# VectorE's order in a transformer layer: both duos' maxima first, then reciprocals and block transposes

## The reference, cut to what matters

```
scores = einsum('bthd,bThd->bhtT', q, k) * (1.0 / sqrt(HD))
scores = where(mask, scores, finfo(float32).min)
out    = einsum('bhtT,bThd->bthd', softmax(scores), v) @ Wo
x = x + tanh(g_xattn[0]) * attention(layernorm(x), ctx, mask)
x = x + tanh(g_ffn[0])   * experts(layernorm(x))
```

## Time and profile before

| what | value |
|---|---|
| median of three runs | 627.38 us |
| the profiled execution | 626.95 us, its span 625.1 us |
| TensorE busy (share of span) | 590.8 us (95%) |
| VectorE busy | 406.8 us (65%) |
| ScalarE busy | 272.5 us (44%) |
| GpSimd busy | 309.0 us (49%) |
| granted TensorE clock, mean | 0.99 of full speed |
| chain that ended last, by engine | PE 71%, DVE 13%, issue 4%, ACT 3%, DMA 3%, SPq 3% |

### The profile page before, as it was taken

How to read it: one execution, slowest core, us unless ns; L and a number is a source line. 1 busy time by engine, 2 the same in 40 slices (tenths; PEclk the granted TensorE clock), 3 DMA queues, 4 the chain that set the end, 5 groups by cost and what they waited for, 6 DMA issues and landing times.

```text
span 625.1 us, 10907 instructions
## 1 busy us (share of the span) xinstructions
PE 590.8 (95%) x2882; PEld 343.7 (55%) x2883; DVE 406.8 (65%) x1266; ACT 272.5 (44%) x713; POOL 309.0 (49%) x272
## 2 busy tenths in 40 slices
PE   3899999999999999999999999889999999999993
PEld 2444465555556555555655555446666656666562
DVE  3578978898998989988899976247353222322231
ACT  2765665566565665665655554212412221122210
POOL 3643554565564698565796655412463222222221
PEclk9999999999999999999999989989999999999998
DMA  8944577586777889687686866999576442333312
GB/s 312 328 111 105 115 163 165 126 183 151 165 148 176 170 191 209 131 181 175 162 205 146 176 150 152 285 323 282 117 165 118 66 57 42 49 51 52 46 23 26
DMA packets 113970, 93.72 MB, mean 150 GB/s; under 512 B 38513, under 2 KB 107505, under 8 KB 113905
## 3 DMA queue, kind: packets, MB, share of 16 engines
q1 hardware_dynamic: 91824, 70.37, 46.5%
q10 hardware_dynamic: 15360, 13.64, 9.9%
q0 software_dynamic: 6720, 8.95, 8.5%
HBM read 27.72 MB, written 12.36 MB: 64 GB/s over the span
## 4 chain that ended last, share of the span: by engine, by line
PE 71%; DVE 13%; issue 4%; ACT 3%; DMA 3%; SPq 3%; ACTq 1%; POOLq 0%; POOL 0%; DVEq 0%
PE ps_s L1625 20%; PE ps_o L1439 12%; PE ps_o L1653 9%; PE ps_s L1393 9%; DVE blocksT L1128 5%; PE ps_a L1449 5%; DVE probs L1116 4%; PE ps_t L1336 4%; PE ps_t L1646 2%; PE ps_o L1406 2%; DMA mask<-mask_dram 2%; ACT probs L720 2%; PE ps_t L1393 2%; PE ps_a L1336 1%; SPq L414 1%
## 5 line engine op out<-in xcount | busy, mean ns | idle before, releaser
L595 POOL TENSOR_TENSOR probs<-probs,inv_sum 128x802 f32<-128x802 f32 x128 | 195.2, 1526 | 138.4 <-DVE inv_sum L1105 137.3
L720 ACT ACTIVATE probs<-probs,neg_max 128x401 f32<-128x401 f32 x256 | 159.4, 625 | 107.3 <-DVE neg_max L1116 105.8
L1625 PE MATMUL ps_s<-w_sb,xgT 128*128 x288 | 137.0, 599 | 3.3 <-issue 3.3
L1116 DVE CUSTOM_DVE_ANT_0 probs<-ps_s,biases 128x401 f32<-128x401 f32 x215 | 116.2, 571 | 21.2 <-PE ps_s L1393 14.4
L1128 DVE STREAM_TRANSPOSE blocksT<-probs 128x832 f32<-128x832 f32 x124 | 129.0, 1040 | 0.4 <-POOL probs L595 0.4
L646 POOL DMA_INDIRECT out_dram<-yg,ids x36 | 56.1, 1559 | 147.3 <-DVE yg L1286 136.8
L1439 PE MATMUL ps_o<-probsT,v_sb 128*64 128x512 f32 x496 | 113.6, 600 | 0.0
L1393 PE MATMUL ps_s<-kT,qT 64*128 64x201 f32 (+1 forms) x860 | 109.6, 350 | 3.5 <-DVE neg_max L1116 2.8
L1393 PEld LDWEIGHTS ps_s<-kT,qT 64*128 64x128 f32 x860 | 84.9, 188 | 44.1 <-issue 27.2
L858 ACT COPY gatedT<-ps_t 128x512 f32<-128x512 f32 x36 | 21.1, 586 | 150.7 <-PE ps_t L1646 150.7
L1276 DVE TENSOR_TENSOR gated<-ps_s,silu 128x512 f32<-128x512 f32 x36 | 24.9, 691 | 91.9 <-PE ps_s L1625 87.5
(11 more groups left out here) (167 smaller groups left out, 515.7 us busy)
## 6 DMA issues: line engine op xcount, KB each, us to landing
probsT<-blocksT SPq DMA_DIRECT2D x276, 96.0 KB
probsT<-blocksT SPq DMA_DIRECT2D x92, 128.0 KB
probsT<-blocksT ACTq DMA_DIRECT2D x96, 96.0 KB
xg_blocks<-x_regrouped SPq DMA_DIRECT2D x156, 32.0 KB, 2.1
probsT<-blocksT ACTq DMA_DIRECT2D x32, 128.0 KB
w_sb<-W1T_dram SPq DMA_DIRECT2D x8, 512.0 KB, 5.1
w_sb<-W2T_dram SPq DMA_DIRECT2D x8, 512.0 KB, 6.2
w_sb<-W3T_dram SPq DMA_DIRECT2D x8, 512.0 KB, 8.0
```

The lines of the kernel that those rows point to most:

```text
L595: pool.tensor_tensor(duo, duo, inv_sum[:, u:u + 2].unsqueeze(2).to_broadcast([P, 2, LASTK]), ALU.mult)\
L720: act.activation(probs[:, b, 0:LASTK], probs[:, b, 0:LASTK], ACT.Exp, bias=neg_max[:, b:b + 1], scale=-1.0, accum_out=sum_exp[:, b:b + 1]) ...
L1116: dve.tensor_tensor_reduce(probs[:, b, 0:LASTK], scores_bank(u)[:, 0:LASTK], biases[:, tile, :], HD ** -0.5, 3e38, ALU.add, ALU.min, neg_m ...
L1625: mm = pe.matmul(bank[:, :], xgT[:, buf, k, :], w_sb[:, bass.ds(expert, 1), (n * KT + k) * FH:(n * KT + k + 1) * FH].squeeze(1), start=(k ...
```

## The change

In steps n = 24, 26, ..., 126 VectorE first takes the maxima of duo n and of duo n+1, four instructions in a row. Then it goes on with the reciprocals of duo n-1, a residual if one is due, and the block transpose of duo n-2; step n+1 has no maxima any more. Steps below 24 stay as they were. No instruction is added or removed, and no other engine's list is changed.

```
--- before.py
+++ after.py
@@ -1167,6 +1167,10 @@
                         normalise(GT + t)
                 if n == 19:
                     dve.wait_ge(tanh_ready, 1)
+                if BURST <= n < DUOS and n % 2 == 0:
+
+                    mask_and_max(n)
+                    mask_and_max(n + 1)
                 if 1 <= n <= DUOS:
                     inverses(n - 1)
                 if n % 8 == 3 and n >= 19:
@@ -1175,7 +1179,7 @@
                     residual((n - 23) // 8, 1)
                 if n == LAST_WO + 1:
                     residual(CHUNKS // 2 - 1, 1)
-                if n < DUOS:
+                if n < BURST:
                     mask_and_max(n)
                 if n + 1 < MASK_DMAS:
                     mask_words(n + 1)
```

## The result

The kernel after takes **655.37 us** (median of 4 runs, 654.82 to 658.37), beside 627.64 for the kernel before in the same job: 1.044 times, 95% interval 1.042 to 1.047; the intervals below are of the same kind. It is slower, as forecast, but by 27.7 us, not 2, and outside the range.

The account below looks back on a forecast made before the run. TensorE bounds most of the time (71% of the chain), VectorE three stretches. A -0.05, B 1.65, C 1.25 and end -0.75 gave +2.1 us, forecasting 629.5 us, range 625.0 to 633.0.

Parts of the forecast that it names:

- A: First stretch where the chain lies on VectorE, ending at the residual of step 55; forecast -0.05 us.
- B: Second stretch where the chain lies on VectorE, ending at the residual of step 87; forecast +1.65 us.
- C: Third stretch where the chain lies on VectorE, schedule work included, ending at the residual of step 119; forecast +1.25 us.
- Step (c): Block transposes newly wait 0.50 us for GpSimd's scaling unless a residual or stage covers it; +0.06 us per stretch.
- Step (b): End of each stretch: the second duo's maxima now precede the residual TensorE waits for; +0.99 us each.
- (a): Start of a stretch: maxima no longer stand behind the previous duo's reciprocals; -1.10 us in A, at most that elsewhere.
- Rival 1: Longer TensorE pauses at the three exits drop its clock, 1.3 us each for two to three: 632.1 to 633.4; chance 0.12.
- Step (d): GpSimd's scalings and scatters ahead of B and C start later, delaying maxima: +0.6 us at B, +0.2 at C.
- Step (e): End of attention: maxima of duo 126 start earlier, bringing the last DMA issues and experts' first matmul forward; -0.75 us.
- Rival 3: Exits at steps 55, 87 and 119 cost nothing because TensorE comes after the residual: 623.4 us; chance 0.14.
- rival 4: TensorE hides all of it, gains and losses falling into slack: 627.4 us; chance 0.14.
- rival 2: GpSimd does not hold VectorE back, so transpose waits and scatter delays are nothing: 626.3 us; chance 0.15.

Follow-up runs that it names:

- e8: Kernel before, with each step's routing stage and schedule part moved ahead of its maxima, right behind reciprocals and residual: 673.45 us (1.072).
- e5: Kernel after, GpSimd scaling only 8 columns per score tile and signalling at once, then doing the full-sized multiplication on a spare buffer: 660.79 us.
- e1: Kernel after, with the second duo's maxima of steps 54, 86 and 118 put back behind the next step's residual: 648.57 us (1.033).
- e2: Kernel after, with the old order restored in steps 48 to 55, 80 to 87 and 104 to 119: 634.16 us (1.010).
- e3: Kernel after, with GpSimd's scaling cut to 8 columns per score tile: 633.00 us, against 633.22 for the kernel before with the same cut.
- e14: Kernel after, with reciprocals ahead of the four maxima, stages directly behind them, and TensorE's stage 8 behind the next burst at the exits: 637.64 us (1.017).
- e7: Kernel after, with routing stages and schedule parts placed between the four maxima and the reciprocals: 645.89 us (1.027).
- e13: Kernel after, with TensorE's stage 8 of steps 55, 87 and 119 behind the next burst: 643.21 us (1.027).
- e6: Kernel after, GpSimd writing a spare buffer by memset, then scaling only 8 columns per score tile and signalling: 645.02 us.

## Why the prediction was wrong

The sum had A at -0.05, B at +1.65 and C at +1.25. By the table A cost 3.5 us (0.2 to 3.7), B 7.3 (4.1 to 11.4) and C 13.5 (11.8 to 25.2).

**Step (c), the cover, failed first.** The prediction said of the transposes' wait that "a routing stage of 0.5 us or more covers that", and took the stage at its old length. That stage is what the scaling holds. I had asked what each moved instruction waits for, and not what runs beside it on another engine in its new place. No term of the sum had it, and no rival. In its place the runs showed held instructions: VectorE was busy 17.5 us longer, moving the small instructions alone costs 45.6 (e8), and holding with hardly a wait of a transpose costs 27.6 (e5).

The kernel before already had the sign. Most of its L962 take 0.15 to 0.19 us, but one that runs beside a scaling takes 0.70 and ends with it:

```profile
379.15 1.52 POOL L595 TENSOR_TENSOR probs<-probs,inv_sum 128x802 f32<-128x802 f32 x1 [2.89 <-DVE inv_sum L1105]
...
380.02 0.70 DVE L962 TENSOR_TENSOR won<-won,rank 128x32 f32<-128x32 f32 x1
```

A look for instructions of one line with unlike lengths would have shown it ahead of the change.

**Step (b), the exits.** The order was right: e1 has its 0.99 back at each. But the residual of step 55 starts 2.38 us later, at 181.85, not where it did. Of that -1.07 is the gain of (a), +0.99 is (b), and 2.3 of the remaining 2.5 are held instructions ahead of it: 0.63 each at L890 and L894, and 0.51 at each of the two pairs of L1004. Residuals 87 and 119 start 9.5 and 23.4 us later, not 1.7 and 3.

**Rival 1** came true, at the wrong price. It stood at 1.3 us an exit and a chance of 0.12, and the forecast took nothing for it, counting on a pause of under 2 us with full bursts behind it. The pauses are 3.5 to 5.0, because the residual is late for another reason, and the low clock alone costs 1.6, 2.3 and 2.0 us at the three exits. The full bursts did not prevent it.

**Step (d)** had its place right and its size wrong. With the old order inside the stretches (e2) the doors and bodies of B and C cost 2.1 and 3.7 us; the forecast was +0.6 and +0.2. I let the last scaling ahead of B begin 1.7 us later. In the kernel after the scaling that the transpose in front of duo 78's maxima waits for starts at 246.42 instead of 239.10, 3.35 us beyond the 3.97 carried in from A, and it holds that transpose for 1.40:

```profile
246.42 1.54 POOL L595 TENSOR_TENSOR probs<-probs,inv_sum 128x802 f32<-128x802 f32 x1
...
248.00 1.04 DVE L1128 STREAM_TRANSPOSE blocksT<-probs 128x832 f32<-128x832 f32 x1 [1.40 <-POOL probs L595]
```

**Step (a)** was right: the maxima of duo 48 start at 159.67 instead of 160.74. Of this gain TensorE keeps 0.58 at step 52. **Step (e)** was wrong: the experts' first matmul starts 28.5 us later, 2.3 more than step 132. TensorE's last out-projection takes 6.62 us there, at a low clock, where it took 3.72 before, so the end gives nothing back. Rival 3 (the exits cost nothing) and rival 4 (all hidden) are out; rival 2 holds only where GpSimd is taken away: there (e3) A gains 0.2 us and the total is level.

**The signs announced**: reciprocals' waits for ScalarE gone, yes; transposes waiting for POOL, yes; L1359's wait over 4, yes, 13.5; bursts' waits for maxima shrinking, no, they grew from 2.8 to 6.5, because VectorE was late. Of the three signs of being wrong none came: the maxima's own waits for scores in the windows of A, B and C are 1.7, 1.9 and 1.9 us, but for 0.3 at the door of A all behind the exit's pause. The signs asked about waits, and the largest loss was in the length of instructions, which none of them looked at.

**Open**: in e14 about 10 us are left, 2.4 of them behind the reciprocals of step 58; the others weren't taken apart. How the loss divides is no sum either: undone one at a time, the holds (e7) give 9.5 us, the pauses (e13) 12.2, the exits' order (e1) 6.8, and the scaling (e3) all of it, because each late thing makes the next one cost more.

## What to carry to other kernels

When an instruction is moved, look at what the other engines do in its new place, not only at what it waits for: here a 0.12 us TENSOR_TENSOR with two SBUF inputs, begun beside GpSimd's TENSOR_TENSOR of 1.52 us, ended when that one ended. Keep small VectorE work away from GpSimd's runs, as the kernel before did by having two maxima and a transpose between reciprocals and stage. And where TensorE waits for a late engine, price the lateness at more than its length once the pause reaches some us: behind pauses of 3.5 to 5.0 us the next 5.73 us of work took 7.4 to 8.0.

## What the hardware did that I had not expected

- **Held instructions.** Forms that grew beside GpSimd's scaling: TENSOR_SCALAR from SBUF to SBUF (L890 139 to 613 ns in the mean, L1004 396 to 585), TENSOR_TENSOR (L966 175 to 553), and in e8 a SCALAR_TENSOR_TENSOR with both inputs in SBUF (1.05 us). The first of each pair of L1004 is held and ends 0.15 us behind the scaling, the others within 0.05 of its end. Forms that ran beside it and didn't grow: BATCH_NORM_STATS2 (L981, 399 in both), TENSOR_REDUCE (L964, 186 in both, once beside a scaling), the 32x32 block transpose (1040 and 1033), the maxima, and the residual, whose first input is in PSUM (733 and 730). The section of the Trainium skill named at e6 (SBUF - State Buffer, Who interferes with whom) draws the line where these rows have it: two SBUF inputs, or a two-port mode. GpSimd's scaling itself stayed at 1.52 us throughout.
- **The clock.** During the 4.99 us pause at the exit of B the granted clock was 0.81 in the mean, in the 8 us of full work behind it 0.69, then 1.00. At the exit of A it was 1.00 during the pause of 3.50 us and 0.77 in the 7.3 us behind it. A pause of 0.77 at the same place left it at 1.00 in the kernel before, and so did two waits of 0.73 and 2.42 us with a burst between them in e13.
